# A causal attention stage with its mask moved into TensorE: eleven row maxima a step instead of sixteen

## The reference, cut to what matters

```python
qkv = einsum('bti,oi->bto', x, W_qkv)          # 16 heads of 8, T = 512, D = 128
q = rope(q); k = rope(k)
scores = einsum('bhqd,bhkd->bhqk', q, k) / sqrt(8)
scores = where(tril(ones(T, T)), scores, -inf)
attn = softmax(scores, axis=-1)
o = einsum('bhqk,bhkd->bhqd', attn, v)
return einsum('bti,oi->bto', o, W_out)
```

## Time and profile before

| | |
|---|---|
| median of three runs | 1834.37 us |
| profiled execution | 1837.55 us, its span 1835.9 us |
| causal attention | from about 1105 to 1547 us of the span |
| TensorE, VectorE, ScalarE, GpSimd busy over the span | 80%, 61%, 46%, 40% |
| custom maxima L668 | 512, 232.7 us busy |
| affine selects L876 | 256, 124.8 us busy |

### The profile page before, as it was taken

How to read it: one execution, slowest core, us unless ns; L and a number is a source line. 1 busy time by engine, 2 the same in 40 slices (tenths; PEclk the granted TensorE clock), 3 DMA queues, 4 the chain that set the end, 5 groups by cost and what they waited for, 6 DMA issues and landing times. The chain is left out here.

```text
span 1835.9 us, 35532 instructions
## 1 busy us (share of the span) xinstructions
PE 1477.3 (80%) x11361; PEld 864.4 (47%) x11361; DVE 1112.6 (61%) x3323; ACT 843.7 (46%) x1410; POOL 733.3 (40%) x1167
## 2 busy tenths in 40 slices
PE   1699999999999867889999915888888985509683
PEld 1255555555555445556666601344444443507462
DVE  3678778778777423633333345688888774517484
ACT  3267677677676634113343302455555554303242
POOL 1133233232332111442323163666665433455387
PEclk8699999999999967999999965899999998559897
DMA  4111110211211043301111122233332211146431
GB/s 114 44 60 36 55 54 28 72 49 29 65 55 33 4 138 47 47 8 40 43 43 43 36 51 67 55 73 78 79 70 67 68 54 47 68 142 188 125 102 52
DMA packets 92595, 115.92 MB, mean 63 GB/s; under 512 B 13018, under 2 KB 76032, under 8 KB 92159
## 3 DMA queue, kind: packets, MB, share of 16 engines
q1 hardware_dynamic: 75518, 91.96, 18.1%
q0 software_dynamic: 16896, 21.69, 5.2%
HBM read 74.00 MB, written 39.34 MB: 62 GB/s over the span
## 5 line engine op out<-in xcount | busy, mean ns | idle before, releaser
L673 DVE TENSOR_REDUCE wm<-wsm 128x16 f32<-128x512 f32 x512 | 330.3, 684 | 130.2 <-PE wsm L415 127.1
L566 ACT ACTIVATE we<-wst 128x1024 f32<-128x1024 f32 x320 | 323.2, 1021 | 127.4 <-PE wst L444 110.4
L668 DVE CUSTOM_DVE_ANT_0 cjunk<-csm,const 128x128 bf16<-128x128 f32 (+3 forms) x512 | 232.7, 486 | 76.8 <-PE csm L415 67.5
L566 ACT ACTIVATE ce<-cst 128x896 f32<-128x896 f32 (+1 forms) x256 | 179.2, 704 | 183.7 <-PE cst L439 182.7
L415 PE MATMUL csm<-cks,cqs 96*128 96x128 bf16 (+3 forms) x512 | 159.6, 319 | 70.5 <-DVE cnm L668 45.2
L415 PE MATMUL wsm<-wks,wqs 96*128 96x512 bf16 x512 | 173.6, 395 | 28.0 <-DMA wks<-qk_parts 17.7
L876 POOL TENSOR_SCALAR_AFFINE_SELECT ce<-ce 128x256 f32<-128x256 f32 x256 | 124.8, 503 | 157.4 <-ACT ce L566 156.6
L444 PE MATMUL wst<-wqs,wks 128*128 128x512 bf16 x512 | 150.7, 386 | 1.2 <-DMA wqs<-wmr 0.7
L1713 DVE TENSOR_TENSOR abhh<-absg,abup 128x512 f32<-128x512 f32 x72 | 49.6, 689 | 152.7 <-ACT absg L1692 152.7
L415 PEld LDWEIGHTS csm<-cks,cqs 96*128 96x128 bf16 x512 | 51.5, 101 | 184.5 <-DVE cnm L668 119.0
L1729 POOL DMA_INDIRECT abxb<-rows,asource x72 | 68.2, 947 | 162.5 <-DVE abys L1720 145.8
(11 more groups left out here) (327 smaller groups left out, 2985.5 us busy)
## 6 DMA issues: line engine op xcount, KB each, us to landing
wqs<-qk_parts SPq DMA_DIRECT2D x96, 96.0 KB
wks<-qk_parts SPq DMA_DIRECT2D x96, 96.0 KB
cqs<-qk_parts SPq DMA_DIRECT2D x96, 96.0 KB
cks<-qk_parts SPq DMA_DIRECT2D x96, 96.0 KB
b1r<-rows SPq DMA_DIRECT2D x40, 194.0 KB, 2.5
qk_parts<-wpt SPq DMA_DIRECT2D x48, 128.0 KB
qk_parts<-cpt SPq DMA_DIRECT2D x48, 128.0 KB
b0r<-rows SPq DMA_DIRECT2D x40, 130.0 KB, 2.3
```

Source lines behind the costliest of these rows:

```text
L566: act.activation(E[:, e_slot(g, i), 0:width], ST[:, (U * g + i) % 2, 0:width], ACT.Exp, scale=SCALE).then_inc(s_ex, 1)
L668: dve.tensor_tensor_reduce(JUNK[:, j % 4, 0:keys], SM[:, j % 2, 0:keys], const["mask_wide"][:, S - keys:S], 1.0, -3e38, ALU.add, ALU.max, ...
L673: dve.tensor_reduce(M[:, n % 2, hs, t, :].rearrange("p (w f) -> p w f", f=DIL), SM[:, j % 2, :].rearrange("p (w i f) -> p w f i", w=NT, f= ...
```

## The change

- The constant table loses the 512 columns of the mask and gains `later` (128x128: -1e30 where the key is later than the query), copied to bf16.
- **Row maxima**: a table `TILES` of eleven entries (query tile, first head, number of heads). The four tiles t = 3 and the four t = 2 stand alone; of t = 1 two heads share a bank (512 columns), of t = 0 all four. TensorE adds the mask of the diagonal block by one more matmul (`later` as weights against the identity). VectorE takes a plain `tensor_reduce` without mask and without accumulator read. `cnm` has two buffers.
- **Scores**: in units 4 to 7 TensorE adds the mask to each diagonal block (two more matmuls a unit), and GpSimd's select falls away; units 0 to 3 keep it. `pv` number 1 waits for ScalarE instead of GpSimd.
- **rows**: ScalarE copies the 12 rows instead of VectorE.
- **Order**: `LATE` is (0, 2), `EARLY` (0, 2, 1, 2, 2, 2). `pv` number 1 moves from unit 2 to 3, and several batch events by one to four units.

```diff
+TILES = [(NT - 1, h, 1) for h in range(HG)] + [(2, h, 1) for h in range(HG)] + [(1, 0, 2), (1, 2, 2), (0, 0, HG)]
...
-    SMU = HG * NT
+    SMU = len(TILES) if causal else HG * NT
-    CUT = 2 if causal else 4
-    LATE = (2, 2) if causal else (2, 2, 2, 0)
-    EARLY = (2, 2, 2, 2, 2, 2) if causal else (1, 2, 2, 1, 2, 2)
+    LATE = (0, 2) if causal else (2, 2, 2, 0)
+    EARLY = (0, 2, 1, 2, 2, 2) if causal else (1, 2, 2, 1, 2, 2)
...
-                put(2, "pv", n - 1, 1)
+                put(3, "pv", n - 1, 1)
...
             def smax(n, g, b, turn, j):        # TensorE
+                sm = SM[:, (SMU * n + j) % 2, :]
+                if causal:
+                    t, first, heads = TILES[j]
+                    keys = (t + 1) * P
+                    for i in range(heads):
+                        h = g * HG + first + i
+                        pe.matmul(sm[:, i * keys:(i + 1) * keys], QS[0:MR0, h, t * P:(t + 1) * P], KS[0:MR0, h, 0:keys],
+                                  start=(i == 0), stop=False, skip_group_check=True)
+                    own = sm[:, 0:heads * keys].rearrange("p (h k) -> p h k", h=heads)[:, :, t * P:keys]
+                    ident = const["ident_b"].rearrange("p (a k) -> p a k", a=1).broadcast_to([P, heads, P])
+                    pe.matmul(own, const["later_b"], ident, start=False, stop=True, skip_group_check=True).then_inc(s_sm, 1)
...
             def scores(n, g, b, turn, i):      # TensorE
+                    masked = i // HG == 1
...
+                        if masked:
+                            m = pe.matmul(st[:, at:at + P], const["ident_b"], const["later_b"],
+                                          start=False, stop=True, skip_group_check=True)
...
-                    pe.wait_ge(s_tri, U * n + HG * (r + 1))
+                if causal and r == 1:
+                    pe.wait_ge(s_ex, U * n + HG * (r + 1))
+                elif causal:
+                    pe.wait_ge(s_tri, HG * (n + 1))
...
             def smax(n, g, b, turn, j):        # VectorE
-                    dve.tensor_tensor_reduce(JUNK[:, j % 4, 0:keys], SM[:, j % 2, 0:keys], const["mask_wide"][:, S - keys:S], 1.0,
-                                             -3e38, ALU.add, ALU.max, NM[:, hs, t:t + 1]).then_inc(s_mx, 1)
+                    t, first, heads = TILES[j]
+                    got = SM[:, (SMU * n + j) % 2, 0:heads * (t + 1) * P].rearrange("p (h k) -> p h k", h=heads)
+                    dve.tensor_reduce(NM[:, n % 2, first:first + heads, t], got, AX.X, ALU.max).then_inc(s_mx, 1)
...
             def scores(n, g, b, turn, i):      # GpSimd
-                if not causal:
+                if not causal or i // HG == 1:
                     return
```

More of the change, by code:

```diff
@@ L169, in slot @@
             if causal:
-                put(2, "pv", n - 1, 1)
+                put(3, "pv", n - 1, 1)
                 put(6, "pv", n, 0)
                 put(3, "evac", n - 1)
-                put(CUT - 1, "maxima", n + 1)
-                put(CUT + 1, "rows", n + 1)
+                put(1, "maxima", n + 1)
+                put(3, "rows", n + 1)
                 put(5, "sel", n - 1)
@@ L178, in slot @@
                     put(1, "part1", b + 1, 1)
[L179 to L180 removed]
+                    put(2, "left1", b + 1, 1)
+                    put(1, "vcopy", b, 2)
                     put(5, "part2", b + 1, 1)
[L182 removed]
+                    put(5, "left2", b + 1, 1)
                     put(7, "parts_out", b + 1, 1)
@@ L413, in smax @@
                     pe.wait_ge(s_mx, SMU * n + j - 1)
-                keys = (t + 1) * P if causal else S
-                pe.matmul(SM[:, j % 2, 0:keys], QS[0:MR0, h, t * P:(t + 1) * P], KS[0:MR0, h, 0:keys], start=True,
-                          stop=True, skip_group_check=True).then_inc(s_sm, 1)
+                sm = SM[:, (SMU * n + j) % 2, :]
[9 more added lines that the diff above has]
+                    pe.matmul(own, const["later_b"], ident, start=False, stop=True, skip_group_check=True).then_inc(s_sm, 1)
+                else:
+                    h, t = g * HG + j // NT, j % NT
+                    pe.matmul(sm, QS[0:MR0, h, t * P:(t + 1) * P], KS[0:MR0, h, :], start=True,
+                              stop=True, skip_group_check=True).then_inc(s_sm, 1)
             def rows(n, g, b, turn):
@@ L437, in scores @@
                 if causal:
+                    masked = i // HG == 1
                     for kb, at, width in cols(i // HG):
                         m = pe.matmul(st[:, at:at + width], KS[:, h, kb * P:(kb + 1) * P], QS[:, h, kb * P:S],
-                                      start=True, stop=True, skip_group_check=True)
+                                      start=True, stop=not masked, skip_group_check=True)
+                        if masked:
+                            m = pe.matmul(st[:, at:at + P], const["ident_b"], const["later_b"],
+                                          start=False, stop=True, skip_group_check=True)
                 elif i < 2 * HG:
@@ L705, in maxima_parts @@
                 for i in range(SPLIT):
-                    last = NM if i == 0 else NR
+                    last = NM[:, n % 2, :, :] if i == 0 else NR[:, :, :]
                     if i < SPLIT - 1:
-                        dve.tensor_copy(part[:, i], last[:, :, :]).then_inc(s_ms, 1)
+                        dve.tensor_copy(part[:, i], last).then_inc(s_ms, 1)
                         dve.wait_ge(s_ms, 4 * n + 2 * i + 1)
@@ L711, in maxima_parts @@
                     if i < SPLIT - 1:
-                        dve.tensor_tensor(to, last[:, :, :], part[:, i], ALU.subtract).then_inc(s_ms, 1)
+                        dve.tensor_tensor(to, last, part[:, i], ALU.subtract).then_inc(s_ms, 1)
                     if i == 0:
                         dve.wait_ge(s_ms, 4 * n + 2)
-            def rows(n, g, b, turn):
-                if not causal:
[L718 to L722, removed]
             def sel(n, g, b, turn):
@@ L765, in _ @@
             walk(dve, dict(ones=ones, norm_stats=norm_stats, norm_rows=norm_rows, proj=proj, rot=rot, join=join, left1=left1, left2=left2, smax=smax, maxima=maxima,
-                           rows=rows, sel=sel, out_proj=out_proj))
+                           sel=sel, out_proj=out_proj))
         @block.gpsimd
@@ L936, in constants @@
         "ident": np.eye(P, dtype=np.float32),
-        "open": np.zeros((P, S - P), np.float32),
-        "mask_q": np.where(p[None, :] <= p[:, None], np.float32(0), -big),
+        "later": np.where(p[:, None] > p[None, :], -big, np.float32(0)),
         "window": np.where(p[:, None] // (P // NT) == np.arange(NT * DIL)[None, :] // DIL, np.float32(3e38), np.float32(-3e38)),
@@ L979, in setup @@
     const = {name: C[:, a:b] for name, (a, b) in at.items()}
-    const["mask_wide"] = C[:, at["open"][0]:at["mask_q"][1]]
-    for i, name in enumerate(("ident", "ones", "before", "dil")):
+    for i, name in enumerate(("ident", "ones", "before", "dil", "later")):
         const[name + "_b"] = CB[:, i * P:(i + 1) * P]
```

34 lines of the change are left out of this document (13 added, 21 removed).

## The result

The changed kernel takes 1812.6 us, median of 4 runs (1808.05 to 1814.98), beside 1836.6 us of the kernel before on the same chip (4 runs): a ratio of 0.9862 (0.9826 to 0.9898), 1.4% faster. The forecast was 1808 us, in a range of 1790 to 1829. The profiled execution took 1812.72 us with a span of 1810.9, so 25 us less than that of before. The size was right, and partly by luck: the experiments show that three of its terms (a bare step, the wait for keys, the batch work) were not, and that their errors cancel.

A forecast was written before the change was run, and what follows sets the result against it. It took a bare step of 10.96 us to be VectorE's and TensorE to bound it afterwards at 9.55. A batch falls from 50.9 to 47.5 us; in all 26 us off, from 1834.37 to 1808 us, range 1790 to 1829.

The forecast's parts named there:

- Maxima on VectorE: Row maxima by plain reductions take 6.2 us a step instead of 7.7; VectorE's step falls from 9.85 to 8.0 us.
- rival D: On VectorE, a plain reduction of packed tiles takes 0.69 us a tile, 8.7 us a step; 1815 us, chance 0.06.
- Masks on TensorE: In TensorE's stream, 19 mask matmuls of 3,072 columns add 1.37 us a step, at 0.057 us per 128 columns.
- rival C: At every mask on TensorE, the 0.113 us weight load isn't hidden, step 11.7 us; 1875 us, chance 0.08.
- TensorE becomes the bound: TensorE's step is 8.2 + 1.37 = 9.55 us, so a bare step falls from 10.96 to 9.55.
- Order: VectorE's splitting lies beside TensorE units without maxima; 2.8 us of TensorE waiting goes to masks and a shorter step.
- Selects: 128 of 256 GpSimd selects go, 62 us of GpSimd, but its idle time covered them: nothing by themselves.
- Key chain: First maximum on the next batch's keys waits for loads queued behind the rows' DMA; 1.8 us a batch.
- Batch work: TensorE's projections and transposes stay at 6.5 us a batch, plus 1.0 where the two banks hold TensorE up.
- The sum: Six batches 20.5 us, three bare steps 3, first stretch 1.5, start 0.5, last steps 0.5; in all 26 us off.
- Rival A: Key chain shortens too and the banks hold nothing up; 44.7 us a batch, 1791 us, chance 0.16.
- Rival B: Key chain waits 3 us and banks cost 2.5 us a batch; 49.7 us a batch, 1822 us, chance 0.16.

The follow-up runs named there:

- the even tables: Changed kernel with maxima spread evenly over units, `LATE` (2, 1), `EARLY` (2, 1, 1, 1, 1, 2), `pv` number 1 in unit 3; ratio 1.0092 to the kernel before.
- second profile: The changed kernel run again without edit, as mark for the follow-up runs; ratio 0.984 to the kernel before, a batch 48.0 us.
- the keys put first: Changed kernel with the next batch's first keys and queries queued on SyncE in unit 0 instead of unit 7, ahead of the rows' DMA; 1799.3 us, ratio 0.9746.

## Why the prediction was right, point by point

- **The bound of the kernel before** was read wrongly. "So the bare step is VectorE's: ... 9.85 us of its work" took the 1.92 us of four maxima as work. By the starts above, the four take 0.61 + 0.48 + 0.34 + 0.21 = 1.64 us; the rest, 0.28 us in four maxima or 1.1 us a step, is small waits at the handing over between two engines over two banks.
- **Maxima on VectorE**, "6.2 us instead of 7.7": the 6.2 was right, by the prices from start to start. The 7.7 was not: without waits the sixteen custom ones are 4 x 1.64 = 6.6. So the change saved 0.4 us of work, not 1.5 (rival D's premise, 0.69 us a tile, isn't met by starts 0.61 apart). What fell besides is the number of hand-overs, from 16 to 11.
- **Masks on TensorE**: the price to the stream, 0.057 per 128 columns, was right, and rival C falls. The Trainium skill (TensorE: Matmul & The Clock Gate, "Back-to-back issue gap") gives 81 ns for such a pair, which the rows of 0.05 to 0.06 us don't show here. What the step pays is less than the columns: 0.54 to 0.7 us for 0.91, by three runs; where the masks stand twice, the wait for VectorE falls, so some of a mask fills such a wait.
- **TensorE becomes the bound**: right in the main. A matmul's busy time runs on until its result is there, so 249.8 of 250 us alone doesn't prove it; that 0.91 us more costs 0.54 and 0.91 us less gives 0.57 shows a bound with some give. The bare step is 9.92 instead of 9.55: small waits are left that were not in the sum. One is the 0.26 us for VectorE at 1471.13, so that 0.47 us pass from the turned rows to the maximum, for which 0.3 were taken; others stand ahead of scores and of `pv` number 1 (0.20 and 0.15 us from the mask to the next start, for 0.06), and `sel` takes 0.86 (0.81).
- **Order**: right in kind, and the change needs it: with the even tables the same change is 0.9% slower than the kernel before, 46 us above the change. The old sixteen maxima in the new order weren't tried, so how the gain divides between fewer tiles and the order stays open.
- **Selects** "nothing": nothing came of them together, but not for the reason given. Their masks cost TensorE 0.2 us a bare step, and as much comes back in the batch.
- **Rows by ScalarE**: nothing, as forecast for the step; nor did the 0.5 us later DMA show in a time.
- **Key chain**, 1.8 us a batch: right in place and mechanism, short in size. The wait is 2.1 us, and three of six times the clock is halved for 3.4 us behind it, which the sum didn't have; in all 3.1 us a batch.
- **Batch work**, 6.5 + 1.0 us: 44.88 less four bare steps of 9.92 is 5.2. Forecast 7.5. This cancels the two errors above: 47.5 + 1.5 (bare steps) + 1.3 (chain) - 2.3 = 48.0, which is what the change had in its second profile. That they cancel is luck. Why the batch work fell by more than a microsecond isn't shown.
- **The sum**: six batches 19.0 us (20.5 forecast), the first steps 3.6 (2.0, the start within it), the last ones 2.8 (3.5): 25.4 at the last `evac`, and 25.0 at the end of the span. The smaller table gave 0.5 us at the first row maximum of the first attention (47.77 for 48.25), but the second attention's first transposes come 1.9 us later than before (1082.50 for 1080.61). So from there to the batches 5.5 us were gained, where 1.5 were forecast; the higher clock of the first stretch may be part of it.
- **Rival A** (44.7 us a batch, 1791 us): the keys put first give nearly its number, 44.9, without the chain that A left out. But A had it as 4 x 9.55 + 6.5, and it is 4 x 9.92 + 5.2: the same cancelling. **Rival B** has a slip: 44.7 + 3 + 2.5 is 50.2 us a batch and not 49.7, so 4 us and not 7, about 1825 us and not 1822.
- **The signs** that were named came: `evac` copies 9.9 us apart in a bare step and 47.75 for four, waits for VectorE 14.4 us (under 20), waits for the keys 12.7 (about 10), one a batch.

## What to carry to other kernels

Where two engines hand small tiles over through two banks, the busy time of neither need be the bound: look at the hand-overs, take an operation's price from start to start where nothing is waited for, and put the producer's other work where the consumer has something long to do. Before a stream is made shorter, look up what loads stand at its fixed places; a queue's order can take the whole gain, and here one moved line was worth more (17 us) than dropping 2,048 columns a step while it stood as it was (8 us).

## What the runs showed of the hardware

- A custom maximum with its accumulator read costs VectorE no more than the plain reduction: 0.61 us from start to start for 512 columns by either.
- A wait of TensorE of about 2 us was followed by 3.4 us at half clock in three of six cases (2.13, 1.89 and 2.54 us waited; behind 2.40, 1.69 and 2.02 it stayed full). The length of the wait doesn't tell them apart; what does stays open.
- Masks with weights of their own, added into a bank between other matmuls, take 0.05 to 0.06 us per 128 columns of TensorE's stream; their loads of 0.1 us don't show in the rows above.
